# First experts write scaled rows to four places per token, the first attention loads them plainly

## The reference

```python
x = x + _L0_attn_ref(_layernorm(x), ...)   # a linear recurrence over 32 sequences of 128
x = x + _L0_ffn_ref(_layernorm(x), ...)    # 32 experts, 4 per token, 128 slots per expert
x = x + _L1_attn_ref(_layernorm(x), ...)   # 16 heads, 16 sequences of 256
x = x + _L1_ffn_ref(_layernorm(x), ...)    # attention, then 8 experts, 1 per token
```

```python
_, idx = jax.lax.top_k(scores + bias[None, :], K)          # K = 4
w = w / jnp.clip(jnp.sum(w, axis=-1, keepdims=True), 1e-12, None)
pos = jnp.take_along_axis(jnp.cumsum(onehot, axis=0) - 1, eid[:, None], axis=1)[:, 0]
valid = pos < C                                            # C = 128
xe = jnp.zeros((E, C, D), x.dtype).at[eid, posc].add(jnp.where(valid[:, None], Xrep, jnp.zeros((), x.dtype)))
h = jax.nn.silu(jnp.einsum('ecd,edi->eci', xe, W1)) * jnp.einsum('ecd,edi->eci', xe, W3)
ye = jnp.einsum('eci,eid->ecd', h, W2)
gflat = jnp.where(valid, w.reshape(-1), jnp.zeros((), x.dtype))
yrows = ye[eid, posc] * gflat[:, None]
out = yrows.reshape(-1, K, D).sum(axis=1)
out = out + jax.nn.silu(X @ sw1.T) * (X @ sw3.T) @ sw2.T
```

## Time and profile before

| | |
|---|---|
| three executions | 1988.16 us median (1965.06 to 1997.38) |
| profiled execution, span | 2019.7 us |
| busy | PE 1449.9 us (72%), DVE 1233.7 (61%), POOL 949.0 (47%), ACT 750.5 (37%) |
| indirect DMAs on POOL | L631 (gathers) 142.1 us in 128, L560 (scatters) 130.9 us in 128 |
| chain that ended last | PE 45%, DVE 25%, no visible wait 10%, POOL 8%, ACT 5% |

### The profile page before, as it was taken

How to read it: one execution, slowest core, us unless ns; L and a number is a source line. 1 busy time by engine, 2 the same in 40 slices (tenths; PEclk the granted TensorE clock), 3 DMA queues, 4 the chain that set the end, 5 groups by cost and what they waited for, 6 DMA issues and landing times.

```text
span 2019.7 us, 28317 instructions
## 1 busy us (share of the span) xinstructions
PE 1449.9 (72%) x8634; PEld 933.4 (46%) x8635; DVE 1233.7 (61%) x2840; ACT 750.5 (37%) x1206; POOL 949.0 (47%) x1080
## 2 busy tenths in 40 slices
PE   3434326478787878778878872899989989984876
PEld 2222214146665656566666671334333333334765
DVE  6877841387876777778778742565746556553332
ACT  1101002144444444444444430445544454541221
POOL 2346476466665656566666442131312213124554
PEclk7555555578887878888888875777876687786777
DMA  4000006100000000000000003000000000001110
GB/s 123 22 24 14 12 7 127 43 5 7 8 8 1 6 6 6 6 6 6 6 6 9 3 3 94 6 9 17 14 10 8 16 8 16 5 11 37 43 42 12
DMA packets 73355, 40.91 MB, mean 20 GB/s; under 512 B 23811, under 2 KB 68716, under 8 KB 73284
## 3 DMA queue, kind: packets, MB, share of 16 engines
q1 hardware_dynamic: 50530, 24.02, 4.3%
q0 software_dynamic: 20384, 11.67, 2.9%
q10 hardware_dynamic: 2370, 4.35, 0.8%
HBM read 31.11 MB, written 23.87 MB: 27 GB/s over the span
## 4 chain that ended last, share of the span: by engine, by line
PE 45%; DVE 25%; issue 10%; POOL 8%; ACT 5%; another core or an unknown queue 3%; DMA 2%; ACTq 1%; POOLq 1%; SPq 0%; DVEq 0%
PE psum L1117 8%; PE psum L1221 6%; PE psum L1242 5%; PE psum L1168 4%; DVE o L1581 3%; PE psum L1251 3%; PE psum L1211 2%; PE psum L1154 2%; POOL yg L631 2%; POOL out L753 2%; PE psum L1126 2%; PE psum L1145 1%; PE psum L1283 1%; DVE rden L1433 1%
## 5 line engine op out<-in xcount | busy, mean ns | idle before, releaser
L1117 PE MATMUL psum<-v,attn 128*128 128x64 f32 x2048 | 293.2, 304 | 25.6 <-ACT aggr L846 17.1
L1117 PEld LDWEIGHTS psum<-v,attn 128*128 128x128 f32 x2048 | 277.2, 217 | 61.9 <-issue 45.7
L1741 DVE TENSOR_REDUCE terms<-psum 128x2 bf16<-128x512 f32 x256 | 170.2, 692 | 94.8 <-PE psum L1242 87.0
L683 POOL TENSOR_SCALAR veps<-meanvar 128x2 f32<-128x2 f32 x32 | 6.1, 192 | 423.4 <-DVE meanvar L1719 423.4
L921 ACT ACTIVATE prob<-psum 128x512 f32<-128x512 f32 x256 | 143.6, 597 | 100.8 <-PE psum L1211 98.6
L1221 PE MATMUL psum<-prob,v 128*32 128x256 f32 x1024 | 172.2, 466 | 0.8 <-ACT pvT L926 0.8
L631 POOL DMA_INDIRECT yg<-ye_dram,routel x128 | 142.1, 1110 | 59.8 <-issue 37.3
L560 POOL DMA_INDIRECT xe_dram<-rows_out,route x128 | 130.9, 1023 | 39.7 <-issue 39.4
L1242 PE MATMUL psum<-k_highT,q_highT 32*128 32x256 bf16 x512 | 127.7, 344 | 29.7 <-DVE terms L1741 27.0
L1126 PE MATMUL psum<-ident,o 128*128 128x128 f32 x256 | 50.1, 360 | 118.8 <-DVE silu_g L1675 82.1
L831 ACT ACTIVATE attn<-psum 128x1024 f32<-128x1024 f32 x128 | 130.1, 1017 | 14.0 <-PE psum L1100 11.2
(11 more groups left out here) (300 smaller groups left out, 3088.7 us busy)
## 6 DMA issues: line engine op xcount, KB each, us to landing
x4n_dram<-x4n SPq DMA_DIRECT2D x16, 256.0 KB, 2.2
w<-in_w POOLq DMA_DIRECT2D x48, 64.0 KB, 2.7
x_in<-in_x SPq DMA_DIRECT2D x8, 256.0 KB, 2.9
xe_dram<-zero_rows SPq DMA_DIRECT2D x8, 256.0 KB, 3.3
x_dram<-x1s SPq DMA_DIRECT2D x8, 256.0 KB
xe_dram<-rows_out,route POOLq DMA_INDIRECT x128
xe<-xe_dram SPq DMA_DIRECT2D x16, 128.0 KB
ye_dram<-ye SPq DMA_DIRECT2D x16, 128.0 KB, 2.2
```

Of the source, the lines that this page charges most:

```text
L1117: mm = pe.matmul(psum[:, 4 + j, (head % HALF) * DV:(head % HALF + 1) * DV], attn[g % RING][:, h, c * SEQ + j * P:c * SEQ + (j + 1) * P], v ...
L1741: dve.tensor_reduce(terms4[:, 0, j, head:head + 2, 6, 0], bank[4 + a2].rearrange("q (b k) -> q b k", b=2), AX, ALU.max, negate=True).then_ ...
```

## The change

- A scattered row gets two more words: `TO`, the row of `yk_dram` to which the expert's output for this token and choice is to go (4 x token + choice), and `SHARE`, its weight. `rows_out` holds four copies of each row, one per choice, because the words differ. `TO` starts from a loaded table (`send_to`) and DVE adds 4096 to it each turn. Empty slots hold `NOWHERE`, which is out of bounds.
- `xe` is loaded whole, in four DMAs. The weights of all experts are loaded once, at the start of the program, by three DMAs of GpSimd. The 16 pairs are written out, PE, ACT and DVE work in three steps on them, ACT scales each output by `SHARE`, and GpSimd scatters each expert's 128 output rows to `yk_dram`, 32 indirect DMAs.
- `yk_dram` (16384 rows) is zeroed at the start of the program by 32 DMAs of SP, ahead of the loads of the attention's weights.
- In the first attention SP loads the 1024 rows of a sequence to `yg` in one DMA. GpSimd adds the four rows and the token in three instructions, which stand behind `length_of(att, 0)`. DVE's `combine` begins with the statistics. `route_dram`, `ye_dram`, `routel`, the gathers and the clearing of `yg` are gone.

```diff
+U1 = 512
+ROW = D + 2
+TO, SHARE = D, D + 1
+NOWHERE = TOK * K0
-        rows_out = two("rows_out", [P, J1, D])
+        rows_out = two("rows_out", [P, J1, K0, ROW])
-        N_CONST_DMA, N_CAST_DMA, N_MADE, N_WEIGHT_DMA = 7, 8, 9, 16
+        N_CONST_DMA, N_CAST_DMA, N_MADE, N_WEIGHT_DMA = 9, 8, 12, 16
+        xe = sb("xe", [P, E0, ROW])
+        w13 = sb("w13", [P, 2, E0, I0])
+        w2 = sb("w2", [P, pairs, D])
...
+                            (rows_out[0][:, :, :, TO].bitcast(U32), a["send_to"][0]), (rows_out[1][:, :, :, TO].bitcast(U32), a["send_to"][1])):
...
+            for n in range(TOK * K0 // U1):
+                sp.dma_start(yk_dram[bass.ds(n * U1, U1)].rearrange("(q r) d -> q (r d)", q=P), zeros[:]).then_inc(yk_zeroed, 16)
...
+            for n in range(4):
+                e = E0 // 4
+                sp.dma_start(xe[:, e * n:e * n + e, :], rows(xe_dram, n * e * CAP, e * CAP, e)).then_inc(s["xe_landed"][n], 16)
...
-                    sp.dma_start(routel[fetch.p][:], rows(route_dram, (fetch.n - 1) * SEQ, SEQ, 2)).then_inc(s["routel_landed"][fetch.p], 16)
+                    sp.dma_start(yg[fetch.p][:].rearrange("q j k d -> q j (k d)"), rows(yk_dram.rearrange("(t k) d -> t (k d)", k=K0), (fetch.n - 1) * SEQ, SEQ, 2)).then_inc(s["yg_landed"][fetch.p], 16)
...
+            pool.dma_start(w13[:, 0, :, :], a["w1"]).then_inc(s["w_landed"], 16)
+            pool.dma_start(w13[:, 1, :, :], a["w3"]).then_inc(s["w_landed"], 16)
+            pool.dma_start(w2[:], a["w2"].rearrange("(n q) d -> q n d", q=P)).then_inc(s["w2_landed"], 16)
+            pool.memset(zero_rows[:, :, 0:TO], 0.0).then_inc(made, 1)
+            pool.memset(zero_rows[:, :, TO].bitcast(U32), NOWHERE).then_inc(made, 1)
+            pool.memset(zero_rows[:, :, SHARE], 0.0).then_inc(made, 1)
+            pool.memset(zeros[:], 0.0).then_inc(made, 1)
...
+            for t in range(pairs):
+                hold(s["ye_made"], t + 1)
+                for e in range(2):
+                    pool.indirect_dma_start(
+                        yk_dram, bass.IndirectOffsetOnAxis(ap=xe[:, 2 * t + e, TO:TO + 1].bitcast(U32), axis=0),
+                        ye[t % 4][:, e, :], None, bounds_check=last_row, oob_is_err=False,
+                    ).then_inc(s["ye_sent"][t % 4], 16)
...
                 if att:
                     length_of(att, 0)
                 if fetch:
+                    hold(s["yg_landed"][fetch.p], 16 * fetch.k)
+                    hold(s["x1l_landed"][fetch.p], 16 * fetch.k)
+                    n = chain.step(pool.tensor_tensor(y_pair[:], yg[fetch.p][:, :, 0:2, :], yg[fetch.p][:, :, 2:4, :], ALU.add))
+                    chain.need(n)
+                    n = chain.step(pool.tensor_tensor(x1l[fetch.p][:], x1l[fetch.p][:], y_pair[:, :, 0, :], ALU.add))
+                    chain.need(n)
+                    if not isinstance(fetch.n, int) or fetch.n > 2:
+                        hold(s["x2_kept_made"], fetch.n - 2)
+                    pool.tensor_tensor(x2[fetch.p][:], x1l[fetch.p][:], y_pair[:, :, 1, :], ALU.add).then_inc(s["x2_made"], 1)
                     hold(s["var3"], fetch.n)
...
-                    act.activation(rows_out[p][:], xn2[p][:], ACT.Copy).then_inc(s["rows_out_made"], 1)
+                    act.activation(rows_out[p][:, :, :, 0:D], xn2[p][:].unsqueeze(2).to_broadcast([P, J1, K0, D]), ACT.Copy).then_inc(s["rows_out_made"], 1)
...
+                    act.activation(ye[t % 4][:, 0, :], bank[4 * (t % 2) + 2][:, 0:D], ACT.Copy, scale=xe[:, 2 * t, SHARE:SHARE + 1])
...
-                dve.wait_ge(s["x1l_landed"][front.p], 16 * front.k)
-                dve.wait_ge(s["yg_landed"][front.p], 16 * 2 * K0 * front.k)
-                for k in range(K0):
-                    for j in range(2):
-                        acc = x1l[front.p] if k == 0 else x2[front.p]
-                        ins = dve.scalar_tensor_tensor(x2[front.p][:, j, :], yg[front.p][:, j, k, :], routel[front.p][:, j, k:k + 1], acc[:, j, :], ALU.mult, ALU.add)
...
                 dve.wait_ge(s["x2_made"], front.n)
```

More of the change, by code:

```diff
@@ L44 @@
 SLOTS0 = E0 * CAP
+U1 = 512
+J1 = U1 // P
+ROW = D + 2
+TO, SHARE = D, D + 1
+NOWHERE = TOK * K0
 class Chain:
@@ L242, in build_program @@
         slot = two("slot", [P, J1 * K0])
-        route = two("route", [P, J1, 2 * K0])
+        route = two("route", [P, J1, K0], U32)
         tanh_a = two("tanh_a", [P, 2 * P])
@@ L277, in build_program @@
         e_hid = two("e_hid", [P, P])
-        ye = two("ye", [P, 2, D])
+        ye = [sb(f"ye{n}", [P, 2, D]) for n in range(4)]
         scope.pop().close()
@@ L457, in turn @@
                 for p in range(2):
-                    sp.wait_ge(s["route_made"], 2 * i + p + 1)
-                    sp.dma_start(rows(route_dram, (2 * i + p) * U1, U1, J1), route[p][:]).then_inc(s["route_stored"][p], 16)
-                for p in range(2):
                     sp.wait_ge(s["x1s_made"], 2 * i + p + 1)
@@ L556, in scatter_rows @@
                 hold(s["rows_out_made"], unit)
-                where = route[p][:].bitcast(U32)
                 for j in range(J1):
@@ L1053, in _ @@
             repeat(pe, T1, turn)
-            def turn(i):
-                for p in range(2):
-                    pe.wait_ge(s["xe_landed"][p], 16 * (i + 1))
+            pe.wait_ge(s["x1s_made"], 2 * T1)
+            pe.wait_ge(s["w_landed"], 32)
+            pe.wait_ge(s["w2_landed"], 16)
+            for at in range(pairs + 2):
+                if at < pairs:
+                    if at % 4 == 0:
+                        pe.wait_ge(s["xe_landed"][at // 4], 16)
+                    wait(pe, s["xeT_made"], at - 1)
@@ L1531, in _ @@
             repeat(dve, T1, turn)
-            def turn(i):
-                for p in range(2):
-                    b = bank[4 * p + 1]
-                    dve.wait_ge(s["e_ab_ps"], 2 * i + p + 1)
-                    dve.wait_ge(s["e_tanh_made"], 2 * i + p + 1)
-                    n = chain.step(dve.scalar_tensor_tensor(e_half[p][:], e_tanh[p][:], 1.0, b[:, 0:P], ALU.add, ALU.mult))
-                    chain.need(n)
-                    dve.scalar_tensor_tensor(e_hid[p][:], e_half[p][:], 0.5, b[:, P:2 * P], ALU.mult, ALU.mult).then_inc(s["e_hid_made"], 1)
-                chain.restart()
-            repeat(dve, T2, turn)
+            for t in range(pairs):
+                b = bank[4 * (t % 2) + 1]
+                dve.wait_ge(s["e_tanh_made"], t + 1)
+                n = chain.step(dve.scalar_tensor_tensor(e_half[t % 2][:], e_tanh[t % 2][:], 1.0, b[:, 0:P], ALU.add, ALU.mult))
+                chain.need(n)
+                wait(dve, s["ye_ps"], t - 1)
+                dve.scalar_tensor_tensor(e_hid[t % 2][:], e_half[t % 2][:], 0.5, b[:, P:2 * P], ALU.mult, ALU.mult).then_inc(s["e_hid_made"], 1)
+            chain.restart()
             dve.drain().then_inc(s["phases"], 1)
@@ L1658, in half @@
                         wait(dve, s["x3_made"], att.n - 2)
-                        chain.step(dve.tensor_copy(x2_kept[att.p][:], x2[att.p][:]))
+                        dve.tensor_copy(x2_kept[att.p][:], x2[att.p][:]).then_inc(s["x2_kept_made"], 1)
                     if tail and g == 1:
```

153 lines of the change are left out of this document (55 added, 98 removed).

## The result

Four executions of the changed kernel had a median of 2020.86 us (2010.28 to 2024.16), against 1982.31 before (four executions, the three of the table and one more): a ratio of 1.0203, 95% interval 1.0147 to 1.0259. Six more, taken later, had 2025.89 against 1982.77, ratio 1.0224 (1.0161 to 1.0287). The kernel became some 2% slower, 39 to 43 us by the medians; that it is slower is clear of the noise, whether by more than 2% is not.

A forecast was written before the change was run, and what follows sets the result against it. A chain of waits between engines bounds it, closed in the first attention by y3 and `x3`. Terms 4 - 1.8 + 3 + 24 + 4.2 - 1.9 - 3 - 16.5 = +12 us: 2000 us, range 1955 to 2043.

The forecast's parts named there:

- the port and the late releases: First attention: GpSimd's later work slows DVE's normalises, +10, or unexplained late DVE waits stay, +16.5; 2010 to 2025, chance 0.22.
- the rival that the wait is not the last: First attention: adds take 1.8 us and `x3` still waits for PE in longer halves; 1981, or 1975; chance 0.14.
- The adds: First attention: DVE waits for GpSimd's three sums behind `o_norm`, `x3` 1.8 us late in 13 halves; +24, range +8 to +43.
- third half: First attention, the half that finishes no sequence: the square behind GpSimd's sums is itself waited for, +4.2 us.
- The start: Program start: more DMA issues and memsets, and 4096 single words of `send_to` loaded; +4 us, range 0 to +12.
- Late releases: First attention: three DVE waits of some 5 us, ascribed to indirect DMAs, would go; -16.5 us, range 0 to -16.5.
- The gathers: First attention: removing GpSimd's indirect loads saves about 1 us in each of three halves where they delayed `o_max`; -3 us.
- Experts: Expert stage to first statistics: 32 scatters end later, but rows come in one load, -1.8; scatter-delayed releases +3, range 0 to +10.
- The rival of the clock: First attention: PE's pause behind y3, from near 4 us on, lowers its clock each half; +56, 2043, chance 0.16.
- The port and the zeros: GpSimd's later work holds DVE's normalises, +10, 2010; or zeroing `yk` delays x loads, +18, 2018, chance 0.06 for the latter.

The follow-up runs named there:

- undisturbed profile: The kernel before, unchanged, executed once more for a second profile: 1997.7 us, span 1996.1, with no wait of DVE, ACT or PE for an unplaced release.
- the scaling last: The kernel before with one edit, GpSimd's scaling of the values `v` moved to the end of its half: 1964.95 us, ratio 0.9905.
- both losses mended: The changed kernel with GpSimd's three adds ahead of the `o_norm` steps and the `send_to` table loaded through a small tile: 1979.91 us, ratio 0.9995.

## Why the prediction was right, and where not

Forecast were 2000 us, +0.6%, with a range of 1955 to 2043; measured were 2021 and 2026, +2.0 and +2.2%: inside the range, 21 to 26 us above the forecast. The mechanism that carries the sum, the adds behind `o_norm`, was right. Of the rest, start, late releases, gathers and clock were mis-sized or false, and all of them made the forecast too low. That the time still lies in the range is in part luck: it is near the chance of 2010 to 2025 given to the port and the late releases, and neither of them brought it there. Two slips stand in the working: 13 x 1.8 is 23.4, not 24, and the 1975 of the rival that the wait is not the last should be 1978.

- *The adds*, +24: right. `x3` was to start 9.8 us behind the norm and does so at 9.88; before it was 7.91 in the undisturbed profile (8.0 by the earlier trace rows). 13 x 1.97 = 25.6. The 128x512 sum was put at 1.27 and took 1.27. The experiment that moves the adds takes it all back; in the one that makes the first add twice `x3` starts 11.24 us behind the norm, 1.36 later. In the third half PE waits 6.05 us instead of 1.77 for the square behind the adds, 4.3 where 4.2 were forecast.
- *The start*, +4: the step that took a word at no more than a 512-byte row, 6.1 us for all, failed. ACT starts 12.7 us later, 11.2 of them by the words. DMA: Bandwidth & Descriptors, section Rules for kernel authors, in the Trainium skill says that a strided last dimension becomes a descriptor for each element; the traces agree, with the 3840 packets that went with the words, and these kept the constants back by 11.2 us.
- *Late releases*, -16.5: false. The step that failed took the rows of one execution for the gathers' doing, because they fell where GpSimd issues indirect DMAs. The second profile of the kernel before and the one of it with the scaling last have the same gathers and no such wait of DVE, ACT or PE. Waits of this kind stand in the second attention of seven of the nine profiles without these gathers, 4.55 us of DVE at 1390.70 in the first profile after, so they come without them too; what causes them is open. This is the largest error of the sum, and it also made the base too long.
- *The gathers*, -3: nothing. With both losses mended the halves are 49.5 us with plain loads and 49.5 with the gathers and DVE's combine.
- *Experts*, -1.8 and +3 for late releases: from the first load of rows to the first statistics it is 64.9 us, and 66.4 in the undisturbed profile of before (305.39 to 371.78): -1.5. The +3 did not come.
- *The rival of the clock*: right in kind, wrong in the point from which it decides. I put that near 4 us of pause; the clock fell behind pauses of 2.27 and 2.61 us in two of the twelve halves, 4 us each, +8, and in the second profile behind 2.08 and 2.10, some 2.3 each. The step that failed is the reading of the 3.45 us pause in the earlier trace rows: I took the eight transposes right behind it for proof that the clock had held. The window that follows them, in the profile of before, has it falling:

```profile
826.00:830.00 4.00, 3.46 (x21) 2.88 (x22) 4.00 (x6) 3.44 (x6) 1.90 (x2) 0.69 0.00 0
```

  So full speed right behind a pause proved nothing here. Pauses of 2.1 to 2.8 us came out either way, and what else decides there is open.
- *The port and the zeros*: neither. The two normalises together take 1.78 us in the mean of the 13 halves, and took 1.78 in the undisturbed profile of before; in the half shown the second took 1.08. The late start is not stretched up to the scatters either (296.2 us from ACT's start to their end, 295.6 before).

Up to the 13th `x3` the traces differ by 50.0 us: 13.4 at the end of the scatters, less 1.9 up to the first statistics, 6.9 from there to the first `x3` (third half and first adds), and 31.7 over the twelve halves, which 12 x 2.0 for the adds and 8 for the clock account for.

## What to carry to other kernels

Work taken from an engine that waits anyway was worth nothing here, and it became a loss where the engine then waited for whoever did it instead. Ask what stands ahead of the new owner's instruction in its own queue: behind some 4 us of small steps three adds cost more than the eight instructions that they replaced, and ahead of those steps nothing. A loss that the trace puts down to no engine is looked for in a second profile before a sum is built on it. Load single words in rows to a tile and spread them from there with an engine.

## What the hardware showed that I had not expected

- Two loads of 2048 single words each moved the constants from 8.2 to 20.9 us; the same table in 64-byte rows and two copies of GpSimd together (0.35 us) cost 1.5.
- DVE and GpSimd hold each other up whole instructions long: `o` takes 4.64 us beside the 4.39 us scaling of the values and 1.22 away from it, and GpSimd's adds 5.4 us among DVE's work and 2.7 while DVE stands still. SBUF — State Buffer, section Who interferes with whom, in the Trainium skill calls it an exclusive lock, and these rows agree.
- The same sums take 1.53 us on DVE and 2.71 on GpSimd while DVE stands still.
- With the same instructions a sequence of the second attention takes from some 30 to 37.4 us within one execution, and the granted clock of that stage was 0.79 and 0.76 in two executions of one kernel.
